# Second sequence's recurrence, projection and h2 in front of the routing list's lanes, slots and expert table

## The chip, the cores and the metric

The kernel runs on one core of a Trainium2 chip. A core has TensorE (PE, matmuls), VectorE (DVE), ScalarE (ACT), GpSimd (POOL) and SyncE (SP, here only a queue that issues DMAs). Each engine works through its own instructions in order and waits on semaphores for the others; all data that they share lies in one on-chip memory, and matmul results in eight banks of PSUM. The metric is the device time of one execution in microseconds, as the median of several runs.

## What is computed

One block with two branches over the same normalised input. Cut to what matters (x is 4 x 512 x 256; 8 experts; 2 picked for each token):

```python
xn = layernorm(x)
# branch 1: gated recurrence, then a feed-forward net
h = rmsnorm(xn); a = sigmoid(h @ w_a + bias); i = sigmoid(h @ w_i); v = h @ w_v
signal = sqrt(1 - a*a) * (i * v)
state[t] = a[t] * state[t-1] + signal[t]          # chunked scan along the sequence
x1 = xn + state @ out_proj_w
h2 = rmsnorm(x1); gate, up = split(h2 @ w_gate_up)
branch1 = x1 + (silu(gate) * up) @ w_down
# branch 2: top-2 of 8 experts for each of the 2048 tokens
logits = xn @ w_router; top-2 and their softmax
branch2 = sum over the picked e of  p_e * (square(relu(xn @ w_fc[e])) @ w_proj[e])
out = x + branch1 + branch2
```

## The kernel before

**Precision.** Nearly every matmul is made of three: each fp32 matrix is split into a rounded "hi" and a remainder "lo", and hi*hi, lo*hi and hi*lo are added in PSUM. Where a weight is split, ACT writes hi (`weights_hi`, L729) and DVE writes lo (`weights_lo`, L1184). For pieces 6 to 10 of the weights the lo half is made without DVE: ACT writes -hi into lo (L731), and a DMA issued on POOL adds the raw weight from DRAM on top (`weights_whole(n)`, L1449). Pieces 6 to 8 are the second halves of w_gate_up and w_down, 9 and 10 the first half of w_fc (Wfc).

**Stages.** The four sequences (b = 0 to 3) first pass through the recurrence's gates (`aiv`), routing logits and statistics. Then come 32 FFN tiles d = 0 to 31, eight for each sequence. A tile is `gate_up(d, 0)` and `gate_up(d, 1)` on PE (12 matmuls of 128x512), Silu on ACT (`gate`, L817), a product on DVE (`up`, L1189, signals `gu_ready`), a split into hi on ACT (`split_gu`, L837) and lo on DVE (L1194), and `down(d)` on PE (12 matmuls of 128x256), one tile later. With tile 8 (`FIRST`) the 39 expert blocks begin to be interleaved; each gathers 128 token rows by an indirect DMA on POOL (`gather`, L1455), transposes them (L615), and multiplies with Wfc and Wpj of its expert. FC, the first product of a block, is called `layer(FC, ...)` in `expert_out(i)`.

**Routing list.** DVE makes it: `blocks(k)` (L1149, L1151), `lanes(0..3)` (L1160), and `experts()` (L1165 to L1170) build comparison matrices; PE multiplies them in `slots()` (L472, 32 small matmuls into bank 6); `block_list()` (L1176, L1178) turns the result into `gather_u` and signals `routed`. POOL waits for `routed` and then issues, in this order, the gathers of blocks 0 to 3 and `weights_whole(10)`. SP waits for it to load the last piece of w_proj, which ACT and DVE split ahead of their part of block 0. PE's first FC, that of block 0, waits for `routed`, for the lo half of the row block (`xg_split`) and for both `w_whole[9]` and `w_whole[10]`.

**Second sequence.** Before tile 8 the second sequence needs `cumulate` and `recur` on DVE (L1056 to L1062), `output_projection(1, ..)` on PE (L444), `add_residual` on DVE (L1070), `squares` on ACT, `root_h2(1)` on POOL (L1423, L1424), `normalise` on ACT (L797), `transpose_h2(1, ..)` on PE (L457) and `split_h2(1)` on ACT and DVE (L1077). Sequence 1 is consumed from tile 8 on.

**What sets the order.** Every engine's program is a list written out by hand. On PE three constants place the extra work of tiles 0 to 7: behind the `gate_up` of tile `SLOTS` stands `slots()`, behind the `down` that follows tile `PROJECT_1` the second sequence's projection, behind that of `TURN_1` its transposes. Two of them share PSUM bank 6 with `slots()`, so a wait keeps them apart: before, the projection waits for `routed`.

Of the kernel before, what the change touches and what calls it, by code (L numbers as in the profile page):

```python
# [14 lines left out]
P = 128  # L15
# [21 lines left out]
def recurrent_moe_block(nc, x, pre_norm_w, w_a, w_i, w_v, out_proj_w, decay_bias, ffn_norm_w,  # L37
                        w_gate_up, w_down, w_router, w_fc, w_proj, out):
    B, S, D = x.shape
    E = w_router.shape[1]  # L40
    FF = w_down.shape[0]
    K = D // P
# [6 lines left out]
    N = T * P  # L49
    ROW = D + E  # L50
# [6 lines left out]
    xh_dram = nc.dram_tensor("xh_dram", [N + P, ROW], F32, kind="Internal").ap()  # L57
# [6 lines left out]
    with ExitStack() as ctx:  # L64
# [215 lines left out]
        PROJECT = {11: 2, 17: 3}  # L280
        TURN = {13: 2, 20: 3}

        SLOTS, PROJECT_1, TURN_1 = 3, 4, 6

        def aside(b):

# [42 lines left out]
        def _(sp):  # L329
# [3 lines left out]
            def load_piece(n):  # L333
                sp.dma_start(pieces[n][1][2], pieces[n][0]).then_inc(w_loaded[n], 16)
# [17 lines left out]
            sp.dma_start(acc_dram[1].rearrange("(n p) d -> p n d", p=P),  # L352
                         zero[:, None, 0:D].to_broadcast([P, T + 1, D])).then_inc(zero_stored, 16)
            sp.dma_start(acc_dram[0][0:N], x.rearrange("b s d -> (b s) d")).then_inc(x_copied, 16)
            sp.wait_ge(w_tok_ready, 1)
            sp.dma_start(xh_dram[0:N, D:ROW].rearrange("(t p) e -> p t e", p=P), w_tok[:, :, :]).then_inc(w_tok_stored, 16)
            sp.wait_ge(aiv_done, 6 * B)
            for n in range(UNDER_SCAN, UNDER_ROUTING):
                load_piece(n)
            sp.wait_ge(routed, 1)  # L360
            sp.wait_ge(experts_ready, 1)
            for n in range(UNDER_ROUTING, ALL):
# [11 lines left out]
        def _(pe):  # L374
# [55 lines left out]
            def output_projection(b, side):  # L430

                if side == 0:
                    pe.wait_ge(rec_ready, K * (b + 1))
                    if b == 0:
                        pe.wait_ge(wo_loaded, 16)
                        pe.wait_ge(hT_split, K * B)
                    elif b == 1:
                        pe.wait_ge(routed, 1)
                        pe.wait_ge(count_taken, 1)
                    else:  # L440
                        pe.wait_ge(*[(gu_ready, d + 1) for d in PROJECT if PROJECT[d] == b][0])
# [22 lines left out]
                nc.tensor.matmul(ps[:, 7, E * T:2 * E * T], ones_bf[:, :], bothv, start=True, stop=True).then_inc(count_done, 1)  # L464

            def slots():
                pe.wait_ge(gu_ready, 3)
                for k in range(TOP):
                    pe.wait_ge(block_ready, k + 1)
                    pe.wait_ge(lane_ready, 2 * k + 2)  # L470
                    for n in range(k * T, (k + 1) * T):
                        last = nc.tensor.matmul(ps[:, 6, 0:NB + 1], at_lane[:, n, :], id_block[:, n, :],  # L472
                                                start=n == 0, stop=n == TOP * T - 1)
                last.then_inc(slots_done, 1)
# [239 lines left out]
        def _(act):  # L714
# [217 lines left out]
            gate(3)  # L932
            weights_hi(9)
            split_gu(3)
            weights_hi(10)
            gate(4)
            weights_hi(11)
            split_gu(4)
            squares(1)
            gate(5)  # L940
            split_gu(5)
            normalise(1)
            weights_hi(12)
            gate(6)
            weights_hi(13)
            split_gu(6)
            split_h2(1)
            weights_hi(14)
            gate(7)
            weights_hi(15)  # L950
# [43 lines left out]
        def _(dve):  # L994
# [294 lines left out]
            split_h2(0)  # L1289
            gated_value(2, 0)  # L1290
            gated_value(2, 1)
            blocks(0)
            blocks(1)
            weights_lo(5)
            gated_value(3, 0)
            lanes(0)
            lanes(1)
            up(0)
            gated_value(3, 1)
            lanes(2)  # L1300
            split_gu(0)
            up(1)
            lanes(3)
            split_gu(1)
            cumulate(1, 0)
            recur(1, 0)
            up(2)
            experts()
            split_gu(2)
            cumulate(1, 1)  # L1310
            up(3)
            block_list()
            recur(1, 1)
            split_gu(3)
            up(4)
            signal(2, 0)
            split_gu(4)
            add_residual(1, 0)
            add_residual(1, 1)
            signal(2, 1)  # L1320
            signal(3, 0)
            up(5)
            signal(3, 1)
            split_gu(5)
            weights_lo(11)
            up(6)
            weights_lo(12)
            split_gu(6)
            weights_lo(13)
            split_h2(1)  # L1330
            weights_lo(14)
            up(7)
            weights_lo(15)
# [52 lines left out]
        def _(pool):  # L1386
# [101 lines left out]
            root_q()  # L1488
            tables()
            root_h2(0)  # L1490
            token_weights()
            for n in range(6, 10):
                weights_whole(n)
            pool.wait_ge(routed, 1)
            for c in range(B):
                pool.wait_ge(xh_stored[c], 16)
# [2 lines left out]
            for i in range(XG):  # L1499
                gather(i)  # L1500
            weights_whole(10)
            root_h2(1)
            pool.wait_ge(x_copied, 16)
            for d in range(FIRST, LAST + 1):
                for v, i in enumerate(blocks_of(d)):
# [52 lines left out]
```

## Time and profile before

| | us |
|---|---|
| median of 3 runs (302.01 to 303.77) | 302.41 |
| the profiled execution | 301.88 |
| its span, first to last instruction | 300.1 |
| PE busy | 282.0 (94%) |
| DVE busy | 194.6 (65%) |
| ACT busy | 170.5 (57%) |
| POOL busy | 158.0 (53%) |

The profile comes from one execution, and its span lies 1.8 us below that execution's own time. The chain that ended last is given to PE for 79% of the span, to DVE for 11% and to DMA for 2%. A timeline row gives start, duration, engine, line, operation and shapes, and in brackets the idle time before it with what ended it. A row may cover several like instructions (x2, x16); matmuls overlap, so what one costs PE is the distance between starts, not its duration. DVE's and ACT's instructions overlap by about 0.1 us in the same way.

### The profile page before, as it was taken

The page shows a single profiled execution, that of the slowest core. Times are in us where ns is not written, and L with a number is a line of the kernel's source. Part 1 is how long each engine was busy: PE and PEld are TensorE (multiplying, and loading weights), DVE is VectorE, ACT ScalarE, POOL GpSimd, SP SyncE. Part 2 cuts the span into 40 slices and gives each one's busy share as a digit, 9 for nine tenths or more (in the row PEclk, how much of TensorE's full clock was granted, in tenths as well). Part 3 has the DMA queues.
Part 4 walks back from the last instruction along what each step waited for, and adds up shares of the span by engine and source line. Part 5 has one row for each costly group of instructions (what it writes and reads, how often), then busy time and mean ns, then how long its engine had stood idle before and what let it go on. Part 6 is the DMA issues. An engine that isn't in the chain of part 4 may idle for free.

```text
span 300.1 us, 5629 instructions
## 1 busy us (share of the span) xinstructions
PE 282.0 (94%) x1826; PEld 249.5 (83%) x1826; DVE 194.6 (65%) x456; ACT 170.5 (57%) x364; POOL 158.0 (53%) x148
## 2 busy tenths in 40 slices
PE   6798999999799899999999999899998999999993
PEld 5587988887689698998988998799988999888893
DVE  3877999979967968865546578645544545443242
ACT  2677868996757744544666454436466555533330
POOL 4797002243561024776676778656876666646500
PEclk9999999999999999999999999999999999999998
DMA  6999990019982010344344353443345344529998
GB/s 174 356 374 382 383 349 0 0 13 261 189 212 41 0 30 28 63 67 70 53 74 69 60 81 62 60 66 56 70 75 76 69 73 54 56 32 161 192 197 292
DMA packets 33371, 36.91 MB, mean 123 GB/s; under 512 B 5184, under 2 KB 30528, under 8 KB 33312
## 3 DMA queue, kind: packets, MB, share of 16 engines
q0 software_dynamic: 13840, 17.20, 35.6%
q1 hardware_dynamic: 16576, 17.25, 17.1%
q10 hardware_dynamic: 2928, 2.10, 2.1%
q8 instruction: 16, 0.26, 0.3%
q14 instruction: 11, 0.09, 0.1%
HBM read 24.68 MB, written 13.96 MB: 129 GB/s over the span
## 4 chain that ended last, share of the span: by engine, by line
PE 79%; DVE 11%; issue 3%; ACT 2%; DMA 2%; SPq 1%; DVEq 0%
PE ps L376 67%; PE ps L615 5%; PE ps L444 5%; DMA X<-in_L_attn_x_dram 2%; ACT h L797 2%; DVE Wpj_lo L1184 2%; DVE gu L1189 1%; DVE guT_lo L1194 1%; PE ps L390 1%; DVE h2T_lo L1077 1%; DVE cum L1057 1%; DVE hT_lo L1031 1%; PE ps L457 1%; DVE gi L1060 1%; DVE stats L1003 0%
## 5 line engine op out<-in xcount | busy, mean ns | idle before, releaser
L1455 POOL DMA_INDIRECT xg<-xh_dram,gather_u x39 | 46.5, 1191 | 52.5 <-DVE picks L1234 40.8
L1464 POOL DMA_INDIRECT acc_dram<-yb,gather_u x39 | 62.2, 1595 | 16.3 <-issue 8.5
L376 PE MATMUL ps<-h2T_lo,Wgu_hi 128*128 128x512 f32 (+1 forms) x132 | 42.9, 386 | 0.0
L376 PE MATMUL ps<-h2T_hi,Wgu_hi 128*128 128x512 f32 (+1 forms) x132 | 41.1, 392 | 1.3 <-DVE h2T_lo L1077 0.9
L376 PE MATMUL ps<-h2T_hi,Wgu_lo 128*128 128x512 f32 (+1 forms) x132 | 40.1, 385 | 0.0
L376 PE MATMUL ps<-Wd_hi,guT_hi 128*128 128x256 f32 x128 | 36.4, 284 | 2.5 <-DVE guT_lo L1194 2.5
L376 PE MATMUL ps<-Wd_hi,guT_lo 128*128 128x256 f32 x128 | 36.2, 283 | 0.0
L376 PE MATMUL ps<-Wd_lo,guT_hi 128*128 128x256 f32 x128 | 36.1, 282 | 0.0
L1251 DVE TENSOR_TENSOR aT_lo<-ps,aT_hi 128x256 fp32r<-128x256 f32 x39 | 16.5, 424 | 29.9 <-ACT aT_hi L859 29.5
L1189 DVE TENSOR_TENSOR gu<-gu,ps 128x512 f32<-128x512 f32 x31 | 21.2, 685 | 21.1 <-PE ps L376 19.0
L817 ACT ACTIVATE gu<-ps 128x512 f32<-128x512 f32 x31 | 18.4, 594 | 22.5 <-PE ps L376 22.4
L376 PEld LDWEIGHTS ps<-h2T_lo,Wgu_hi 128*128 128x128 f32 x132 | 24.5, 188 | 4.7
L376 PEld LDWEIGHTS ps<-h2T_hi,Wgu_lo 128*128 128x128 f32 x132 | 24.5, 188 | 4.5
L837 ACT ACTIVATE guT_hi<-gu 128x512 fp32r<-128x512 f32 x31 | 19.5, 628 | 15.3 <-DVE gu L1189 15.3
L376 PEld LDWEIGHTS ps<-Wd_hi,guT_hi 128*128 128x128 f32 x128 | 24.3, 190 | 4.6 <-DVE guT_lo L1194 3.5
L859 ACT ACTIVATE aT_hi<-ps 128x256 fp32r<-128x256 f32 x39 | 14.9, 382 | 21.8 <-PE ps L615 21.8
L1242 DVE TENSOR_TENSOR xgT_lo<-ps,xgT_hi 128x256 fp32r<-128x256 f32 x39 | 16.4, 421 | 15.6 <-ACT xgT_hi L845 15.5
L845 ACT ACTIVATE xgT_hi<-ps 128x256 fp32r<-128x256 f32 x39 | 14.9, 383 | 18.5 <-PE ps L615 18.5
L376 PEld LDWEIGHTS ps<-Wd_lo,guT_hi 128*128 128x128 f32 x128 | 24.3, 190 | 1.0
L1194 DVE TENSOR_TENSOR guT_lo<-gu,guT_hi 128x512 fp32r<-128x512 f32 x31 | 21.3, 687 | 5.8 <-ACT guT_hi L837 5.4
L376 PEld LDWEIGHTS ps<-h2T_hi,Wgu_hi 128*128 128x128 f32 x132 | 21.6, 189 | 3.4 <-DVE h2T_lo L1077 1.4
L376 PEld LDWEIGHTS ps<-Wd_hi,guT_lo 128*128 128x128 f32 x128 | 24.3, 190 | 0.0
(184 smaller groups left out, 679.3 us busy)
## 6 DMA issues: line engine op xcount, KB each, us to landing
X<-acc_dram POOLq DMA_DIRECT2D x8, 512.0 KB, 10.8
acc_dram<-zero SPq DMA_DIRECT2D x1, 2176.0 KB, 16.3
Wgu_raw<-in_L_attn_w_gate_up_dram SPq DMA_DIRECT2D x4, 512.0 KB, 9.4
Wfc_raw<-in_L_ffn_w_fc_dram SPq DMA_DIRECT2D x4, 512.0 KB, 13.6
xh_dram<-X ACTq DMA_DIRECT2D x4, 512.0 KB, 7.8
Wpj_raw<-in_L_ffn_w_proj_dram SPq DMA_DIRECT2D x4, 512.0 KB, 5.5
X<-in_L_attn_x_dram SPq DMA_DIRECT2D x3, 512.0 KB, 7.2
out_dram<-X SPq DMA_DIRECT2D x3, 512.0 KB, 5.4
```

Of the source, the lines that this page charges most:

```text
L376: return nc.tensor.matmul(dst, lhs, rhs, start=start, stop=stop, skip_group_check=group)
L444: last = nc.tensor.matmul(ps[:, aside(b) + side, (j % 2) * D:(j % 2 + 1) * D], dec[b][:, k, j * P:(j + 1) * P], Wo[:, k, :], start=k == 0, ...
L615: last = nc.tensor.transpose(ps[:, bank, k * P:(k + 1) * P], src[:, k * P:(k + 1) * P], ident[:, :])
L817: A.activation(gu[d % 2][:, :], ps[:, gu_bank(d), :], ACT.Silu).then_inc(sg_ready, 1)
L837: A.activation(guT[d % 2][0][:, :], gu[d % 2][:, :], ACT.Copy).then_inc(gu_hi, 1)
L845: A.activation(xgT[i % 2][0][:, :, :].rearrange(flat), ps[:, T1, 0:D], ACT.Copy).then_inc(xg_hi, 1)
L1189: V.tensor_tensor(gu[d % 2][:, :], gu[d % 2][:, :], ps[:, gu_bank(d) + 1, :], ALU.mult).then_inc(gu_ready, 1)
L1194: V.tensor_tensor(guT[d % 2][1][:, :], gu[d % 2][:, :], guT[d % 2][0][:, :].bitcast(F32), ALU.subtract).then_inc(gu_split, 1)
L1242: V.tensor_tensor(xgT[i % 2][1][:, :, :].rearrange(flat), ps[:, T1, 0:D], xgT[i % 2][0][:, :, :].rearrange(flat).bitcast(F32), ALU.subtrac ...
L1251: V.tensor_tensor(aT[i % 2][1][:, :, :].rearrange(flat), ps[:, T2, 0:D], aT[i % 2][0][:, :, :].rearrange(flat).bitcast(F32), ALU.subtract) ...
L1455: pool.indirect_dma_start(out=xg[i % XG][:, :], out_offset=None, in_=xh_dram, in_offset=bass.IndirectOffsetOnAxis(ap=gather_u[:, i:i + 1], ...
L1464: pool.indirect_dma_start(out=acc_dram[i % 2], in_=yb[i % YB][:, :], in_offset=None, compute_op=ALU.add, out_offset=bass.IndirectOffsetOnA ...
```

## The change

The routing list moves back and the second sequence forward. On PE the projection of sequence 1 goes behind tile 3 (from 4), its transposes behind tile 5 (from 6), and `slots()` behind tile 6 (from 3). Bank 6 is now first the projection's: it waits for `gu_ready` 3 in place of `routed`, and `slots()` waits for the four halves of h2T. DVE's, ACT's and POOL's lists follow; SP stores the token weights behind three of the four w_proj loads. No arithmetic is added or taken away. The diff, with its repeated lines cut:

```diff
-        SLOTS, PROJECT_1, TURN_1 = 3, 4, 6
+        SLOTS, PROJECT_1, TURN_1 = 6, 3, 5
...
                     elif b == 1:
-                        pe.wait_ge(routed, 1)
+                        pe.wait_ge(gu_ready, 3)
...
             def slots():
-                pe.wait_ge(gu_ready, 3)
+                pe.wait_ge(h2T_split, 2 * K)
...
-            blocks(0)
-            blocks(1)
             weights_lo(5)
             gated_value(3, 0)
-            lanes(0)
-            lanes(1)
+            cumulate(1, 0)
+            recur(1, 0)
             up(0)
...
             token_weights()
-            for n in range(6, 10):
-                weights_whole(n)
+            root_h2(1)
+            weights_whole(9)
             pool.wait_ge(routed, 1)
...
             weights_whole(10)
-            root_h2(1)
             pool.wait_ge(x_copied, 16)
```

On DVE, what stands from the third FFN product on to the list. In these rows gu, guT are tiles of the FFN, L1056 to L1062 the recurrence, L1165 to L1170 `experts()`, L1176 and L1178 `block_list()`. Before:

```order
L1189 TENSOR_TENSOR gu_130<-gu_130,ps 128x512
L1165 TENSOR_TENSOR past<-blk_end,lane 128x320
L1167 TENSOR_REDUCE expert_f<-past 128x40
L1168 TENSOR_SCALAR expert_u<-expert_f 128x40
L1169 TENSOR_SCALAR one_of<-past 128x40
L1170 TENSOR_TENSOR one_of<-past 128x40x7
L1194 TENSOR_TENSOR guT_lo<-gu_130,guT_hi 128x512
L1056 TENSOR_SCALAR dec_106<-dec_106 128x512
L1057 SCALAR_TENSOR_TENSOR cum<-restart,dec_106 128x512
L1189 TENSOR_TENSOR gu_131<-gu_131,ps 128x512
L1176 TENSOR_SCALAR row_of<-ps,lane_p 128x40
L1178 SCALAR_TENSOR_TENSOR gather_u<-ps,row_of 128x40
```

The same engine in the changed kernel, from the third product to the split of that tile:

```order
L1189 TENSOR_TENSOR gu_130<-gu_130,ps 128x512
L1060 SCALAR_TENSOR_TENSOR gi_110<-cum,gi_110 128x512
L1062 SCALAR_TENSOR_TENSOR dec_106<-dec_106,gi_110 128x512
L1149 TENSOR_TENSOR at_block<-step_64,hi_f 128x640
L1151 TENSOR_TENSOR id_block<-at_block,token 128x640
L1194 TENSOR_TENSOR guT_lo<-gu_130,guT_hi 128x512
```

And, three tiles later, from the product of tile 5 to the list and what follows it:

```order
L1189 TENSOR_TENSOR gu_131<-gu_131,ps 128x512
L1077 SCALAR_TENSOR_TENSOR h2T_lo<-ps,ffn_w,h2T_hi 128x512 x2
L1194 TENSOR_TENSOR guT_lo<-gu_131,guT_hi 128x512
L1047 SCALAR_TENSOR_TENSOR gi_111<-gain_134,gi_111 128x512 x2
L1176 TENSOR_SCALAR row_of<-ps,lane_p 128x40
L1178 SCALAR_TENSOR_TENSOR gather_u<-ps,row_of 128x40
L1047 SCALAR_TENSOR_TENSOR gi_112<-gain_135,gi_112 128x512 x2
L1189 TENSOR_TENSOR gu_130<-gu_130,ps 128x512
L1184 TENSOR_TENSOR Wfc_lo<-Wfc_raw,Wfc_hi 128x1024
L1194 TENSOR_TENSOR guT_lo<-gu_130,guT_hi 128x512
L1184 TENSOR_TENSOR Wfc_lo<-Wfc_raw,Wfc_hi 128x1024
L1184 TENSOR_TENSOR Wpj_lo<-Wpj_raw,Wpj_hi 128x1024 x2
```

The recurrence now stands ahead of all the list's work, and the list (L1176, L1178) has gone from between the products of tiles 3 and 4 to just ahead of the product of tile 6.

On PE, around `slots()` in the changed kernel (L457 are the transposes of sequence 1, the rows behind it one side of tile 6 and the next, L472 `slots()`):

```order
L457 MATMUL ps<-ident_52,h2_187 128x128 x8
L376 MATMUL ps<-h2T0_hi_126,Wgu_hi_89 128x512 x2
L376 MATMUL ps<-h2T0_lo_127,Wgu_hi_89 128x512 x2
L376 MATMUL ps<-h2T0_hi_126,Wgu_lo_90 128x512 x2
L376 MATMUL ps<-h2T0_hi_126,Wgu_hi_89 128x512 x2
L376 MATMUL ps<-h2T0_lo_127,Wgu_hi_89 128x512 x2
L376 MATMUL ps<-h2T0_hi_126,Wgu_lo_90 128x512 x2
L472 MATMUL ps<-id_block_142,at_lane_140 128x40 x32
L376 MATMUL ps<-Wd_hi_92,guT1_hi_138 128x256
```

Before, `slots()` stood three tiles earlier, with neither projection nor transposes ahead of it.

On POOL, the difference between the two lists ahead of the gathers (L1432 to L1438 are `token_weights()`, L1423 and L1424 `root_h2(1)`, L1449 the adding DMAs):

```order
+L1449 DMA Wgu_lo<-in_L_attn_w_gate_up_dram 128x2x512 x2
+L1449 DMA Wd_lo<-in_L_attn_w_down_dram 128x4x256
 L1432 TENSOR_TENSOR prob<-prob,q_77 128x16 x2
 L1435 TENSOR_TENSOR tmp<-mask,prob 128x128
 L1436 TENSOR_TENSOR lg_146<-mask,prob 128x128
 L1438 TENSOR_TENSOR w_tok<-tmp,lg_146 128x128
-L1449 DMA Wgu_lo<-in_L_attn_w_gate_up_dram 128x2x512 x2
-L1449 DMA Wd_lo<-in_L_attn_w_down_dram 128x4x256
+L1423 TENSOR_SCALAR sn<-ssq 128x4
+L1424 TENSOR_TENSOR rn_88<-sn,minus_half 128x4
 L1449 DMA Wfc_lo<-in_L_ffn_w_fc_dram 128x4x256
 L1455 DMA xg_169<-xh_dram,gather_u 128x264
```

The token weights and the root now stand between the adding DMAs. Behind these rows nothing moved: the gathers of blocks 0 to 3 and then the second Wfc_lo DMA, `weights_whole(10)`, all behind `routed`.

## Rows read from the trace of the kernel before

**Rows 1.** Busy time by stretch: PE, PEld, DVE, ACT, POOL, clock, DMA share, GB/s

```profile
66.00:105.00 39.00, 35.17 (x226) 29.90 (x225) 33.84 (x50) 27.46 (x46) 13.19 (x11) 1.00 0.63 136
...
105.00:110.00 5.00, 5.00 (x39) 4.69 (x38) 2.74 (x10) 1.80 (x5) 1.09 (x1) 1.00 0.10 29
```

**Rows 2.** Chain of waits, 66 to 106 us: start, us, what

```profile
101.18 0.60 DVE gu L1189
101.77 2.27 DVE Wpj_lo L1184 x2
104.05 0.34 DVE xgT_lo L1242
```

**Rows 3.** ScalarE's timeline, 66 to 74 us: start, us, operation, idle before

```profile
69.43 0.63 ACT L837 ACTIVATE guT_hi<-gu 128x512 fp32r<-128x512 f32 x1 [1.89 <-DVE gu L1189]
...
71.87 0.57 ACT L817 ACTIVATE gu<-ps 128x512 f32<-128x512 f32 x1
```

**Rows 4.** VectorE's timeline, 56 to 81 us

```profile
56.45 0.82 DVE L1149 TENSOR_TENSOR at_block<-step,hi_f 128x640 f16<-128x640 f16 x1
...
58.05 0.82 DVE L1149 TENSOR_TENSOR at_block<-step,hi_f 128x640 f16<-128x640 f16 x1
...
66.38 0.69 DVE L1042 TENSOR_TENSOR gi<-gi,ps 128x512 f32<-128x512 f32 x1 [1.01 <-PE ps L376]
...
72.77 0.69 DVE L1060 SCALAR_TENSOR_TENSOR gi<-cum,gi 128x512 f32<-128x512 f32 x1
...
74.63 0.66 DVE L1189 TENSOR_TENSOR gu<-gu,ps 128x512 f32<-128x512 f32 x1
...
79.74 0.25 DVE L1176 TENSOR_SCALAR row_of<-ps,lane_p 128x40 f32<-128x40 f32 x1
80.03 0.20 DVE L1178 SCALAR_TENSOR_TENSOR gather_u<-ps,row_of 128x40 uint32<-128x40 f32 x1
```

**Rows 5.** TensorE's timeline, 75 to 105 us

```profile
75.47 0.98 PE L472 MATMUL ps<-id_block,at_lane 128*128 128x40 f16 x32
77.56 0.39 PE L376 MATMUL ps<-Wd_hi,guT_hi 128*128 128x256 f32 x1 [1.11 <-DVE guT_lo L1194]
...
84.26 3.62 PE L444 MATMUL ps<-Wo,dec 128*128 128x256 f32 x16
...
90.48 0.28 PE L376 MATMUL ps<-Wd_hi,guT_hi 128*128 128x256 f32 x1
...
94.66 0.28 PE L376 MATMUL ps<-Wd_hi,guT_hi 128*128 128x256 f32 x1
...
99.71 0.28 PE L376 MATMUL ps<-Wd_hi,guT_hi 128*128 128x256 f32 x1
...
104.52 0.51 PE L376 MATMUL ps<-Wfc_hi,xgT_hi 128*128 x2 [0.97 <-DVE xgT_lo L1242]
```

**Rows 6.** GpSimd's timeline, 80 to 88 us

```profile
80.51 1.30 POOL L1455 DMA_INDIRECT xg<-xh_dram,gather_u  x1 [0.60 <-DVE gather_u L1178]
...
86.26 1.47 POOL L1449 DMA_DIRECT2D Wfc_lo<-in_L_ffn_w_fc_dram  x1
```

**Rows 7.** DMA issues from 86.2 to 87 us: KB each, us to landing

```profile
Wfc_lo<-in_L_ffn_w_fc_dram POOLq DMA_DIRECT2D x1, 512.0 KB, 6.1
```

**Rows 8.** GpSimd's timeline later, shortest and longest gather

```profile
140.00 0.98 POOL L1455 DMA_INDIRECT xg<-xh_dram,gather_u  x1 [1.83 <-PE ps L615]
...
187.59 1.91 POOL L1455 DMA_INDIRECT xg<-xh_dram,gather_u  x1 [0.58 <-issue]
```

**Rows 9.** TensorE's timeline, 2 to 11 us

```profile
2.82 4.45 PE L380 MATMUL ps<-before,ones_bf 128*128 128x128 bf16 x40 [2.82 <-POOLq L1403]
...
9.89 0.83 PE L380 MATMUL ps<-before,ones_bf 128*128 128x128 bf16 x12
```

**Rows 10.** Busy time by stretch at the end, columns as in rows 1

```profile
295.00:295.50 0.50, 0.12 (x2) 0.00 (x0) 0.50 (x2) 0.00 (x0) 0.00 (x0) 1.00 1.03 363
...
298.50:299.00 0.50, 0.00 (x0) 0.00 (x0) 0.00 (x0) 0.00 (x0) 0.00 (x0) 0.50 0.68 236
```

More of the change, by code:

```diff
@@ L354, in _ @@
             sp.dma_start(acc_dram[0][0:N], x.rearrange("b s d -> (b s) d")).then_inc(x_copied, 16)
-            sp.wait_ge(w_tok_ready, 1)
-            sp.dma_start(xh_dram[0:N, D:ROW].rearrange("(t p) e -> p t e", p=P), w_tok[:, :, :]).then_inc(w_tok_stored, 16)
             sp.wait_ge(aiv_done, 6 * B)
@@ L359, in _ @@
                 load_piece(n)
+            sp.wait_ge(w_tok_ready, 1)
+            sp.dma_start(xh_dram[0:N, D:ROW].rearrange("(t p) e -> p t e", p=P), w_tok[:, :, :]).then_inc(w_tok_stored, 16)
             sp.wait_ge(routed, 1)
@@ L934, in _ @@
             split_gu(3)
+            squares(1)
+            gate(4)
             weights_hi(10)
-            gate(4)
+            split_gu(4)
+            normalise(1)
+            gate(5)
             weights_hi(11)
-            split_gu(4)
-            squares(1)
-            gate(5)
+            split_h2(1)
             split_gu(5)
-            normalise(1)
             weights_hi(12)
@@ L946, in _ @@
             split_gu(6)
-            split_h2(1)
             weights_hi(14)
@@ L1291, in _ @@
             gated_value(2, 1)
-            blocks(0)
-            blocks(1)
             weights_lo(5)
             gated_value(3, 0)
-            lanes(0)
-            lanes(1)
+            cumulate(1, 0)
+            recur(1, 0)
             up(0)
             gated_value(3, 1)
-            lanes(2)
             split_gu(0)
             up(1)
-            lanes(3)
+            cumulate(1, 1)
             split_gu(1)
-            cumulate(1, 0)
-            recur(1, 0)
             up(2)
-            experts()
+            recur(1, 1)
+            blocks(0)
             split_gu(2)
-            cumulate(1, 1)
+            blocks(1)
+            lanes(0)
             up(3)
[L1312 to L1317, printed above, removed]
             add_residual(1, 0)
             add_residual(1, 1)
+            split_gu(3)
+            lanes(1)
+            up(4)
+            lanes(2)
+            split_gu(4)
+            lanes(3)
+            experts()
+            up(5)
+            split_h2(1)
+            split_gu(5)
+            signal(2, 0)
             signal(2, 1)
+            block_list()
             signal(3, 0)
-            up(5)
             signal(3, 1)
-            split_gu(5)
+            up(6)
             weights_lo(11)
-            up(6)
+            split_gu(6)
             weights_lo(12)
-            split_gu(6)
             weights_lo(13)
-            split_h2(1)
             weights_lo(14)
@@ L1490, in _ @@
             root_h2(0)
+            for n in range(6, 9):
+                weights_whole(n)
             token_weights()
-            for n in range(6, 10):
-                weights_whole(n)
+            root_h2(1)
+            weights_whole(9)
             pool.wait_ge(routed, 1)
```

## The prediction, made before the changed kernel was run

> **What bounds the kernel now.** I read the busy times by stretch first. From 66 to 105 us, where tiles 0 to 7 run, PE is busy 35.17 of 39.00 us, so 3.8 us of PE idle time lie there; DVE is busy 33.84 us [rows 1]. In the next stretch PE is busy 5.00 of 5 us and DVE 2.74 [rows 1]: from the first expert block on PE alone sets the time. So the question is only when PE gets out of tiles 0 to 7, and the marker is its first FC, which starts at 104.52 us [rows 5]. Every microsecond that this start moves should move the end, since behind it there is no PE idle time that could absorb it.
>
> The chain of waits says what held that start: not a DMA and not the list, but DVE's queue, 0.60 us for a product, 2.27 us for two Wpj_lo, 0.34 us for xgT_lo [rows 2]. The list itself was early: `gather_u` ended at 80.03 + 0.20 = 80.23 us [rows 4], and the DMA issued behind the four gathers, `weights_whole(10)`, started at 86.26 us [rows 6] and landed 6.1 us later [rows 7], at 92.4 us. That left 12.1 us of slack to FC. The change spends this slack.
>
> **Part 1: the recurrence in front of the list, what it gives.** In the trace `down(2)` on PE starts at 77.56 us behind 1.11 us of waiting for guT_lo [rows 5]. In the changed order DVE takes at 66.38 us [rows 4] the same gated value, then without a lane in between guT_lo(0) and the product of tile 1, at 0.60 us each [rows 2]; the product ends at about 68.3. ACT then goes through the same pieces as before, from guT_hi(1) to the end of the third Silu, 69.43 to 71.87 + 0.57, 3.0 us [rows 3]: 71.4. So the third product starts at 71.5 in place of 74.63 [rows 4]. Behind it stand, ahead of guT_lo(2), the product itself 0.60, half a recurrence 74.63 - 72.77 = 1.86, and `blocks(0)` 58.05 - 56.45 = 1.60 [rows 4]: 75.6, guT_lo(2) ends at 76.2 and `down(2)` starts at 76.3. That is 1.3 us earlier than before. I find no wait behind it in tiles 3 to 5: the projection needs `recur(1, 1)`, over by 74, and each later guT_lo has about 1 us or more in hand.
>
> **Part 2: when the list is ready.** From `down(2)` on PE now runs, ahead of `slots()`: `down(2)`, 1.4; projection and one tile's gate_up, 90.48 - 84.26 = 6.22; a down and a gate_up, 94.66 - 90.48 = 4.18; a down, the transposes and a gate_up, 99.71 - 94.66 = 5.05 [rows 5]. Sum 16.9, so `slots()` starts at 93.2 in place of 75.47 [rows 5]. It takes 0.98 us [rows 5], some 0.1 us to DVE, and the two list instructions take 80.23 - 79.74 = 0.49 us [rows 4]. `routed` comes at 94.8, against 80.23: 14.6 us later. The new wait of `slots()` for h2T costs nothing, since a tile's gate_up, over 2.7 us, lies between the transposes and it, and DVE has both lo halves by about 92. What is queued behind the waiting `block_list()` on DVE are two signals and all the weight splits; DVE waits some 0.4 us there.
>
> **Part 3: what hangs on the list.** POOL waits for `routed`, then issues four gathers and the adding DMA. From `gather_u` to the start of that DMA the trace shows 86.26 - 80.23 = 6.03 us [rows 4, 6], then 6.1 us to landing [rows 7]. `w_whole[10]` thus comes at 94.8 + 6.0 + 6.1 = 106.9, and FC, which waits for it, starts at about 107.1. Before: 104.52. **Loss: 2.6 us.** The two bounds of the POOL term: a gather takes between 0.98 and 1.91 us in this trace [rows 8], and 0.3 us lie between two; four then take 5.1 to 8.8 us, and the DMA would be issued 5.4 to 9.1 us after `routed`. I keep 6.03, since it is these same four gathers under the same busy DVE and beside the same load of the last w_proj piece. This gives FC +2.0 to +5.7 us.
>
> On the price of that DMA the Trainium skill speaks against me. For 512 KB the row shows 6.1 us [rows 7]. "DMA: Bandwidth & Descriptors", section "Anatomy of one DMA", gives about 2.0 us fixed plus the bytes over 436 GB/s, an estimate of 3.2 us; by it the DMA would land at 104.0 and FC be held by something else, the first rival below. The trace's value decides here.
>
> **Part 4: the rest.** The token weights (POOL) now stand between adding DMAs and need `blocks(0)`, and the root of h2 stands behind them; by the count of part 1 both end near 85, about a microsecond before ACT uses the root. The store of the token weights is issued by SP behind three loads that wait only for the gates' last matmul, near 66, and is long over by 94.8. The last w_proj piece lands some 6 us after `routed`, at 101, and ACT splits it by 102, so that ACT's and DVE's part of block 0 is behind it but ahead of 105. These edits cost nothing as long as `w_whole[10]` is later; without that cover they are the first rival. PE's time saved in part 1 is given back in the wait before FC and is in the sum already. PE's work is unchanged.
>
> **Sum.** Profiled execution 301.88 us, span 300.1, plus 2.6: 304.5. The median of the runs shown is 302.41, 0.53 us above that execution: 305.0 us.
>
> **Rivals.**
>
> *A. The adding DMA is hidden, and DVE's queue decides as before.* Behind `gather_u` DVE still has five instructions of 0.60 us and six weight splits of 2.27 / 2 = 1.14 us, then xgT_lo 0.34 us [rows 2]: 94.8 + 3.0 + 6.8 + 0.3 = 104.9, and FC 0.13 us later, at 105.1, or 0.6 us later than before. Time 303.0. For it: DVE is busy for 87% of this stretch already, and its work is only reordered. Against it: POOL's path would have to be 2 us shorter than the same instructions took in the trace.
>
> *B. PE's clock falls in the new wait.* By DVE's queue the last gate_up ahead of FC ends at about 103.9, so PE stands still for some 3.2 us before 107.1. At the end of the trace PE's last matmul ends at 295.1 with the granted clock at 1.00, and from 298.5 on the granted clock is 0.50, 1.2 of 2.4 GHz [rows 10]. What a low level costs: 40 small matmuls at the start take 4.45 us, 12 of the same later 0.83 us [rows 9], 111 ns against 69 ns each, so 1.7 us over a ramp of that length. Time 305.0 + 1.7 = 306.7. The Trainium skill's "TensorE: Matmul & The Clock Gate", section "Why this matters for your kernels", asks for no longer idle gaps between bursts of matmuls, since the clock then goes back to half; the rows at the end of the trace agree.
>
> *C. Faster.* If neither POOL nor DVE holds FC, PE comes to it by its own work: `slots()` ends at 94.2, a down and a gate_up 4.18, then what lay between 99.71 and 104.52 without the last wait of 0.97 us [rows 5], 3.84 us: 102.2, which is 2.3 us earlier. Time 300.1. It decides only if `w_whole[10]` has landed by 102.2, within 7.4 us of `routed`, where the trace shows 12.1, and if DVE has also caught up 3 us.
>
> **How the numbers follow.** Forecast 0.68, A 0.15, B 0.12, C 0.05. A measurement of this kernel can tell about 0.5%, 1.5 us, from no change: 300.9 to 303.9. The forecast and B are slower by more, A is within it, C is faster; I move 0.02 from slower to the middle for a `routed` that comes a microsecond earlier than my count. Faster 0.05, same 0.17, slower 0.78. The range starts a little under A, 302.8, and goes to 307.9, which holds B and nearly the upper bound of the gathers (305.0 + 3.1); C and rows beyond that are left out.
>
> **What would show it.** In the changed profile: `down(2)` near 76.3; L472 near 93.2; `gather_u` near 94.8; the L1449 DMA behind the fourth gather near 100.8; FC near 107, its idle time put down to that DMA or, since a wait is named by what came last, to an engine long done; the stretch from FC on busy on PE as before, and a span near 302.7. If PE's idle time ahead of FC is under 1.5 us and xgT_lo ends right before it, A was right. If small matmul spacings behind FC are doubled, B. If `routed` comes before 90, part 2 is wrong, and with it all else.

## The result: 310.5 us, 2.3% slower, beyond the range

The changed kernel takes 310.51 us in the median of 4 runs (308.77 to 311.19), beside 302.37 us (302.01 to 303.77) for the kernel before. The ratio is 1.0227, with a 95% interval of 1.0176 to 1.0278. It is slower, as forecast, but by 8.1 us where 2.6 were forecast, and the time lies above the range.

The profiled execution took 310.57 us, its span is 308.5 us, 8.4 us over the span before. Two of the changed kernel's waits of TensorE between 60 and 125 us (what waited and for whom: us in total, times, longest):

```profile
PE ps L376 <- DMA Wfc_lo<-in_L_ffn_w_fc_dram: 4.4, 1, 4.4
...
PE ps L376 <- DVE gu L1189: 2.2, 1, 2.2
```

The first is new, for the adding DMA, ahead of FC. The second stands ahead of the last gate_up before FC; the kernel before waited 0.39 us for the same product at this place. The chain of waits between 90 and 116 us shows what the first is made of:

```profile
96.03 0.84 PE ps L472 x32
...
97.19 0.21 DVE gather_u L1178
...
97.69 1.29 POOL xg L1455
...
99.28 1.92 POOL xg L1455
...
101.50 1.44 POOL xg L1455
...
103.24 1.96 POOL xg L1455
105.20 5.66 DMA Wfc_lo<-in_L_ffn_w_fc_dram
110.86 0.34 issue
111.20 2.90 PE ps L376 x9
```

`slots()` (L472), the list (L1178), four gathers (L1455), the DMA of 5.66 us, and then TensorE. In the kernel before, the same stretch of the chain was VectorE's queue [rows 2]. TensorE's own timeline of the changed kernel, against [rows 5] of before:

```profile
61.93 0.62 PE L376 MATMUL ps<-h2T_hi,Wgu_hi 128*128 128x512 f32 x2
```

```profile
78.89 0.39 PE L376 MATMUL ps<-Wd_hi,guT_hi 128*128 128x256 f32 x1 [1.05 <-DVE guT_lo L1194]
...
95.87 0.98 PE L472 MATMUL ps<-id_block,at_lane 128*128 128x40 f16 x32
...
105.13 0.70 PE L376 MATMUL ps<-h2T_hi,Wgu_hi 128*128 128x512 f32 x2 [2.18 <-DVE gu L1189]
...
111.20 0.76 PE L376 MATMUL ps<-Wfc_hi,xgT_hi 128*128 x2 [4.45 <-DMA Wfc_lo<-in_L_ffn_w_fc_dram]
```

The first row is the surprise. Tile 0 starts at 61.93 us, where it started at 59.31 us in the kernel before, and nothing that the change touches runs that early. So there are three losses, and each can be read off by taking the stretches apart. The first is the start: tile 0 comes 2.6 us late. The second is the stretch from tile 0 to the first FC: 111.20 - 61.93 = 49.3 us, where it was 104.52 - 59.31 = 45.2, so 4.1 us more. The third is from FC to the end of the span: 308.5 - 111.2 = 197.3, where it was 195.6, so 1.7 us more. For the first, the chain of waits of the changed kernel between 8 and 17 us begins with the load of the second sequence's input:

```profile
3.31 7.65 DMA X<-in_L_attn_x_dram
...
13.13 1.20 DVE hT_lo L1031 x2
```

In the profile of before the same piece of the chain is 6.64 us long, 1.0 us less. For the third, these are busy times by stretch, columns as in [rows 1], the granted clock the last but two:

```profile
16.00:18.00 2.00, 2.00 (x6) 1.61 (x5) 1.93 (x13) 0.90 (x2) 1.42 (x3) 0.50 1.09 359
...
111.00:112.00 1.00, 0.80 (x4) 0.80 (x5) 0.00 (x0) 0.00 (x0) 0.00 (x0) 0.63 0.00 0
112.00:113.00 1.00, 1.00 (x5) 0.95 (x5) 0.00 (x0) 0.14 (x1) 0.00 (x0) 0.50 0.00 0
113.00:114.00 1.00, 1.00 (x4) 0.65 (x3) 0.51 (x3) 0.24 (x1) 0.00 (x0) 0.50 0.00 0
114.00:115.00 1.00, 1.00 (x6) 0.88 (x5) 0.02 (x1) 0.39 (x1) 0.44 (x1) 0.66 0.00 0
115.00:116.00 1.00, 1.00 (x9) 0.95 (x8) 0.94 (x2) 0.00 (x0) 0.61 (x1) 1.00 0.00 0
```

At 16 and at 112 us the granted clock stands at 0.50, 1.2 of 2.4 GHz; the first time behind a wait of 2.00 us of TensorE for hT_lo, the second behind the waits ahead of FC. So a clock fall belongs to the start too. An estimate from the four rows of 111 to 115 us: what they lack of full speed adds up to 0.37 + 0.50 + 0.50 + 0.34 = 1.7 us, which is the third loss. The runs below take these three losses apart.

### The profile page after: what moved, and what is told of

The parts are those of the page before. It is cut to its first block, busy times and chain, and to the rows that moved or that the text cites. A ratio compares the mean times of both kernels' runs of the same rounds, so it can differ in the third digit from the quotient of the medians.

```text
span 308.5 us, 5630 instructions
## 1 busy us (share of the span) xinstructions
PE 284.9 (92%) x1826; PEld 251.9 (82%) x1826; DVE 194.0 (63%) x456; ACT 170.7 (55%) x364; POOL 160.0 (52%) x148
## 4 chain that ended last, share of the span: by engine, by line
PE 76%; ACT 7%; DVE 5%; DMA 4%; issue 3%; POOL 2%; SPq 1%; DVEq 0%; ACTq 0%
PE ps L376 65%; PE ps L615 5%; PE ps L444 4%; DMA X<-in_L_attn_x_dram 2%; POOL xg L1455 2%; DMA Wfc_lo<-in_L_ffn_w_fc_dram 2%; ACT h L797 1%; PE ps L390 1%; PE ps L457 1%; ACT gain L785 1%; DVE hT_lo L1031 1%; ACT gain L780 1%; ACT Wgu_hi L729 1%; ACT h2T_hi L805 1%; DVE h2T_lo L1077 0%
## 5 line engine op out<-in xcount | busy, mean ns | idle before, releaser
L1455 POOL DMA_INDIRECT xg<-xh_dram,gather_u x39 | 48.2, 1237 | 53.3 <-DVE picks L1234 25.8
L1247 DVE TENSOR_TENSOR act_e<-ps,act_e 128x256 f32<-128x256 f32 x39 | 16.6, 425 | 14.9 <-ACT act_e L865 11.2
L865 ACT ACTIVATE act_e<-ps 128x256 f32<-128x256 f32 x39 | 15.0, 386 | 18.2 <-PE ps L376 15.8
```

Of the source, the lines that this page charges most:

```text
L865: A.activation(act_e[i % 2][:, :], ps[:, FC, 0:D], ACT.Relu).then_inc(relu_done, 1)
L1247: V.tensor_tensor(act_e[i % 2][:, :], ps[:, FC, 0:D], act_e[i % 2][:, :], ALU.mult).then_inc(act_ready, 1)
L1455: pool.indirect_dma_start(out=xg[i % XG][:, :], out_offset=None, in_=xh_dram, in_offset=bass.IndirectOffsetOnAxis(ap=gather_u[:, i:i + 1], ...
```

## The experiments

Since executions differ by up to 3 us at the start, traces are compared by three marks: the start of tile 0 on TensorE, the start of the first FC (Wfc_hi, xgT_hi), and the end of the span. The kernel before has 45.2 us between the first two and 195.6 us between the last two in its first trace; in a second one, below, they are 45.2 and 196.0, so a difference of 0.4 us behind FC says nothing.

### The kernel before once more

> The kernel before, unchanged, for a second trace beside the others of this call. In the first trace of the changed kernel everything up to tile 0 already ran 2.66 us late: the load of X of the second sequence landed 1.0 us later, TensorE stood still 2.00 us ahead of hT_lo in place of 0.90, and its clock was 0.50 from 16 to 18 us. Theory S (start-up varies from run to run): in this trace too the second product of lo weights may start anywhere from 13.3 to 14.4 us, and the clock of 16 to 18 us may be 1.00 or 0.50. Theory C (the changed program causes it): this trace repeats 13.3 us and a clock of 1.00.

305.32 us and a span of 303.5. The input load of its chain took 7.42 us, 0.8 us more than in the first trace; one short VectorE instruction behind it (L1008) took 0.77 us in place of 0.17. And TensorE's timeline at the start reads:

```profile
12.07 0.63 PE L376 MATMUL ps<-hT_hi,Waiv_lo 128*128 128x512 f32 x2
14.69 0.73 PE L376 MATMUL ps<-hT_lo,Waiv_hi 128*128 128x512 f32 x2 [1.98 <-DVE hT_lo L1031]
...
16.63 1.06 PE L376 MATMUL ps<-hT_lo,Waiv_hi 128*128 128x512 f32 x2
```

The wait on hT_lo is 1.98 us, as in the changed kernel, and the two matmuls at 16.63 take 1.06 us in place of 0.62: the clock. Tile 0 starts at 62.29 us and FC at 107.50, 45.2 us behind; from there to the end it takes 196.0 us. Theory S holds: the late start happens without the change too. In 13 runs of the kernel before that stood beside these it took 302.09 to 305.3 us.

### The changed kernel once more

> The changed kernel, unchanged, timed against the kernel before. Theory S: the time lies between 306 and 311 us and the start-up differs between its executions. Theory C: 310.5 us again, with hT_lo's product at 14.4 us and a clock of 0.50 from 16 to 18 us. Both expect the first FC 14 us behind gather_u (111.20 - 97.39 = 13.8 in the first trace).

310.62 us (308.99 to 311.87), ratio 1.0259 with an interval of 1.0204 to 1.0315. This time the trace has tile 0 at 59.87 us, nearly on time, FC at 109.46, 49.6 us behind it, and the end 197.4 us behind FC. The adding DMA was again issued 7.8 us behind the list, and FC came 6.3 us behind that in place of 6.0. So 4.1 to 4.4 us up to FC and 1.7 to 1.9 us behind it (1.3 to 1.5 against the second trace of before) belong to the change, and a start that is late by 0 to 3 us does not. The expectation's 13.8 us from the list to FC became 109.46 - 95.31 = 14.2.

### e1: the adding DMA ahead of the wait for the list

```diff
             weights_whole(9)
+            weights_whole(10)
             pool.wait_ge(routed, 1)
...
                 gather(i)
-            weights_whole(10)
```

> The changed kernel with one step moved: weights_whole(10), the adding DMA on Wfc's second piece, is issued on GpSimd ahead of the wait for routed, right behind weights_whole(9), in place of behind the four gathers. Main theory (FC waits for that DMA, and the wait costs 4.4 us and lets the clock fall once): FC starts right behind xgT_lo, at the place DVE's queue sets, some 3.6 us earlier relative to gather_u than in the changed kernel (10.2 us behind it), and the clock stays at 1.00 there, worth another 1.5 us. Time 5 us below the changed kernel, some 305.5. Rival (FC is held by the gathers or by the last w_proj piece as well): under 2 us gained.

304.95 us (302.67 to 307.17), ratio 1.006 with an interval of 1.0021 to 1.0098; 5.7 us under the changed kernel in the medians. In the traces, from tile 0 to the end, it is 244.0 against 246.6 and 247.0 us, 2.5 to 3.0 us less; the rest of the 5.7 is not taken apart here, and the start varies in both. FC in this trace:

```profile
102.36 0.70 PE L376 MATMUL ps<-h2T_hi,Wgu_hi 128*128 128x512 f32 x2 [2.17 <-DVE gu L1189]
...
104.96 0.79 PE L376 MATMUL ps<-Wfc_hi,xgT_hi 128*128 x2 [0.75 <-DVE xgT_lo L1242]
```

It starts at 104.96 us, 45.8 us behind tile 0 (59.16), right behind xgT_lo, and the DMA is gone from its wait. This is rival A of the prediction, to the tenth: VectorE's queue then sets FC, 0.6 us later than in the kernel before. The second half of the expectation failed. The clock fell all the same:

```profile
102.00:103.00 1.00, 0.64 (x3) 0.58 (x4) 1.00 (x2) 0.63 (x1) 0.44 (x1) 1.00 0.00 0
103.00:104.00 1.00, 1.00 (x5) 0.47 (x3) 1.00 (x2) 0.00 (x0) 0.00 (x0) 0.80 0.49 135
...
105.00:106.00 1.00, 1.00 (x5) 1.00 (x6) 0.42 (x1) 0.00 (x0) 0.00 (x0) 0.50 0.00 0
...
109.00:110.00 1.00, 1.00 (x5) 0.90 (x4) 0.49 (x2) 0.00 (x0) 0.29 (x1) 0.50 0.12 25
110.00:111.00 1.00, 1.00 (x9) 1.00 (x8) 0.39 (x1) 0.01 (x1) 0.00 (x0) 0.79 0.42 126
```

It is at 1.00 until 103, falls there and stays at 0.50 until 110, and from FC to the end it takes 198.2 us, 2.6 more than before. The only idle time of TensorE of more than 0.1 us between 92 us and the fall is the 2.17 us ahead of the last gate_up before FC; the 0.75 us for xgT_lo come behind the fall. So the wait for the DMA is not needed for the clock to fall: it can fall right behind the gap of 2.2 us in front of it, which the changed kernel has too. In the seven traces with neither this gap nor a wait for the DMA (before twice, e3, e4, e6, e7, e8) the clock did not fall there. Of the six traces with this gap of 2.2 us the clock fell before FC in three (here, and below in e9 and e10), behind the DMA's wait in two (the changed kernel's), and not at all in e2.

### e2: unused matmuls in the wait

`keep_clock(56, 7)` puts 56 matmuls of 128 columns, whose result nobody reads, into PSUM bank 7 ahead of the waits of FC.

```diff
                     else:
+                        keep_clock(56, 7)
                         pe.wait_ge(routed, 1)
```

> The changed kernel with 56 small matmuls of 128 columns, whose result is not used, on TensorE ahead of the first FC's wait for the adding DMA. They take about 3.1 us at full clock and fit in the wait. Main theory: FC starts when it did (13.8 us behind gather_u), but the stretch behind it runs at 1.00 in place of 0.66, and the time falls by 1.5 to 1.7 us. Rival (the clock in that stretch is not what costs): no change within 0.5 us.

309.38 us (307.21 to 310.21). In the trace FC comes 109.18 - 59.23 = 49.95 us behind tile 0, a little later than without them (49.3 to 49.6), and the end only 195.9 us behind FC, where the changed kernel took 197.3 and 197.4. The clock is at 1.00 through 105 to 115 us. The medians differ by 1.2 us, but the times of the two kernels overlap (4 runs each), and the start may be a part of it; the traces give 1.4 to 1.5 us for the clock behind FC, less the 0.4 to 0.7 by which FC came later. The matmuls do not show as the cause of that delay: behind them TensorE still waited 0.94 us for the DMA, which landed 6.3 us after its issue, where the changed kernel had 5.7 and 6.0. Why it took longer is open.

### e3: the DMA early and VectorE's splits later

On VectorE the product of tile 7 and xgT_lo of block 0 move ahead of the four Wpj splits; with e1's edit:

```diff
             weights_lo(12)
-            weights_lo(13)
-            weights_lo(14)
             up(7)
-            weights_lo(15)
-            weights_lo(16)
...
+                        if i == 0:
+                            weights_lo(13)
+                            weights_lo(14)
                         if v == 1:
                             up(d)
+                        if i == 1:
+                            weights_lo(15)
...
                         block_weight(i)
+                        if i == 1:
+                            weights_lo(16)
```

> The changed kernel with two edits: weights_whole(10) ahead of the wait for routed, as in the run before, and on VectorE the product of tile 7 and xgT_lo of block 0 ahead of the four Wpj splits, which follow inside blocks 0 and 1. Main theory (with the DMA out of the way FC is set by VectorE's queue): FC starts at TensorE's own arrival, 42 to 43 us behind tile 0 (changed kernel 49.3 to 49.6, kernel before 45.2), the 2.2 us of idle time ahead of gate_up(8) go, the clock stays at 1.00, and the time is 299 to 300.5 us, under the kernel before. Rival (ScalarE's w_proj pieces or the gathers come next): FC at 44 to 46 us behind tile 0 and 302 us or more.

302.72 us (302.34 to 306.7), ratio 1.001 with an interval of 0.9961 to 1.0058. FC starts at 102.58 us, 42.5 us behind tile 0 (60.06), 2.7 us sooner than in the kernel before: TensorE's own arrival, which the prediction's rival C had put at 102.2 - 59.3 = 42.9. The idle time ahead of gate_up(8), the last before FC, is gone and the clock stays at 1.00 there. But the end comes 198.3 us behind FC, 2.7 more than before, so the whole gain is given back:

```profile
109.98 0.47 PE L376 MATMUL ps<-Wpj_hi,aT_hi 128*128 x2 [1.70 <-DVE Wpj_lo L1184]
```

The first PJ now waits 1.70 us for the last Wpj split, and the rest of what was given back lies in the gaps just ahead of it, where VectorE is busy without a pause. Only part of the main theory held.

### e4: VectorE's edit on the kernel before

> The kernel before with the VectorE edit alone: product of tile 7 and xgT_lo of block 0 ahead of the four Wpj splits. If VectorE's queue alone set the first FC there, as its chain of waits says, FC comes at most 2.3 us earlier (42.9 us behind tile 0) and the time falls to 300.5 to 301.5. If the splits are then late for the first PJ, the gain is given back there and the time stays at 302.5 to 303.

304.27 us (302.83 to 307.01), ratio 1.0035 with an interval of 0.9997 to 1.0072: no gain. FC 43.5 us behind tile 0 and the end 198.1 us behind FC: 1.7 us gained, 2.5 given back, with a wait of 1.69 us of the first PJ for Wpj_lo. Both expectations were too kind; the chain of waits named VectorE, and relieving its queue at one place loaded it at the next.

### e5: VectorE's edit on the changed kernel, the DMA left where it is

> The changed kernel with the VectorE edit alone; the adding DMA stays behind the four gathers. FC has to wait for that DMA as before. Theory P (VectorE's two-input splits slow the issue of the gathers on GpSimd, 1.92 and 1.96 us in the changed kernel against 0.95 to 1.43 before): with four splits of 1.2 us gone from that stretch the later gathers take 0.95 to 1.3 us, the adding DMA is issued 6.0 us behind gather_u in place of 7.8 to 8.0, and FC comes 12.2 us behind it in place of 13.8 to 14.1. Rival (the gathers' price has another cause): 7.8 to 8.0 us and 13.8 us again.

310.02 us in two runs. What it is for are the gathers, and this is GpSimd's timeline:

```profile
95.07 1.29 POOL L1458 DMA_INDIRECT xg<-xh_dram,gather_u  x1 [8.46 <-DVE gather_u L1178]
96.66 1.92 POOL L1458 DMA_INDIRECT xg<-xh_dram,gather_u  x1 [0.30 <-issue]
98.88 1.44 POOL L1458 DMA_INDIRECT xg<-xh_dram,gather_u  x1 [0.30 <-issue]
100.62 0.95 POOL L1458 DMA_INDIRECT xg<-xh_dram,gather_u  x1 [0.30 <-issue]
101.57 1.47 POOL L1452 DMA_DIRECT2D Wfc_lo<-in_L_ffn_w_fc_dram  x1
```

The first three gathers are the same as in the changed kernel's chain above, 1.29, 1.92 and 1.44 us; the fourth takes 0.95 us in place of 1.96. What VectorE did beside the gathers, first in the changed kernel (from the second gather on) and then here (beside the fourth):

```profile
99.11 1.22 DVE L1184 TENSOR_TENSOR Wfc_lo<-Wfc_raw,Wfc_hi 128x1024 fp32r<-128x1024 f32 x1
...
100.89 1.22 DVE L1184 TENSOR_TENSOR Wfc_lo<-Wfc_raw,Wfc_hi 128x1024 fp32r<-128x1024 f32 x1
102.03 2.35 DVE L1184 TENSOR_TENSOR Wpj_lo<-Wpj_raw,Wpj_hi 128x1024 fp32r<-128x1024 f32 x2
104.30 0.68 DVE L1189 TENSOR_TENSOR gu<-gu,ps 128x512 f32<-128x512 f32 x1
104.90 2.35 DVE L1184 TENSOR_TENSOR Wpj_lo<-Wpj_raw,Wpj_hi 128x1024 fp32r<-128x1024 f32 x2
```

```profile
99.41 0.68 DVE L1189 TENSOR_TENSOR gu<-gu,ps 128x512 f32<-128x512 f32 x1
101.26 0.42 DVE L1242 TENSOR_TENSOR xgT_lo<-ps,xgT_hi 128x256 fp32r<-128x256 f32 x1 [1.17 <-ACT xgT_hi L845]
```

In the changed kernel a pair of 1024-wide splits, with two inputs in on-chip memory, ends inside the fourth gather (103.24 to 105.20), and the next pair begins inside it; here VectorE stands idle for 1.17 us ahead of xgT_lo, which covers the fourth gather (100.62 to 101.57) but for its last 0.3 us. The adding DMA is issued 101.57 - 94.77 = 6.8 us behind the list in place of 105.20 - 97.39 = 7.8. Theory P expected 6.0; the fourth gather fell as it said, and the second stayed at 1.92 us, because a split still runs at its start. FC comes 13.2 us behind the list in place of 13.8. But with VectorE's work out of the way TensorE is sooner at its wait and stands in it for 6.15 us, the clock is at 0.50 until past FC by 4 us, and the first PJ waits 1.36 us for its weights, much as in e3: the end comes 199.8 us behind FC, 4.2 more than before, so that the time is no lower.

The rows allow more than "VectorE is busy". The second gather starts at 99.28, inside a split that ends at 99.11 + 1.22 = 100.33, 1.05 us later, and takes 1.92; the third starts at 101.50 with 0.61 us of a split left and takes 1.44, though splits run beside all of it; the fourth has 1.14 us left of one and takes 1.96. So what counts is how much is left of the instruction that VectorE is in when the gather starts. All 546 gathers of the 14 traces fit this. Where VectorE was idle at their start, or in an instruction with an input in PSUM, they took 0.94 to 1.09 us (354). Where it was in one with two inputs that both lie in the on-chip memory (192), they took 0.95 us and what was left of it less 0.1 us, each within 0.14 us. By it the changed kernel's four gathers had 0.30, 1.05, 0.61 and 1.14 us left at their starts, those of the kernel before 0.31, 0.55, 0.33 and nothing:

```profile
82.11 1.43 POOL L1455 DMA_INDIRECT xg<-xh_dram,gather_u  x1 [0.30 <-issue]
...
85.31 0.95 POOL L1455 DMA_INDIRECT xg<-xh_dram,gather_u  x1 [0.30 <-issue]
```

Less 0.1 us each, these add 0.89 us to four times 0.95 us before and 2.70 us in the changed kernel. The difference, 1.8 us as an estimate, is the 1.8 us by which the DMA was issued later.

### e6: the start

On the kernel before, the split of the first hT goes ahead of the second sequence's statistics, which wait for a load:

```diff
             normalise_first(1)
-            statistics(1)
             split_h(0)
+            statistics(1)
             split_router()
```

> The kernel before with hT_lo's split of the first sequence ahead of the second sequence's statistics on VectorE. Theory (start-up spread: the statistics wait for a load that lands 1 us earlier or later, TensorE waits behind them, and its clock falls in some executions): hT_lo's product starts at 12.5 us, its wait is under 0.5 us, and the spread of the times shrinks from 302.0 to 305.3 to under 1.5 us, median about 301.5 to 302.5. Rival (the spread comes from elsewhere): the spread stays at 3 us.

301.56 us (301.18 to 302.92), ratio 0.9934 with an interval of 0.9899 to 0.9969. The same place in the trace:

```profile
11.85 0.63 PE L376 MATMUL ps<-hT_hi,Waiv_lo 128*128 128x512 f32 x2
12.31 0.63 PE L376 MATMUL ps<-hT_lo,Waiv_hi 128*128 128x512 f32 x2
```

No wait is left ahead of the lo product, where it was 0.90 to 2.00 us, and 25 runs of the kernel before beside it spread from 302.06 to 306.0 us, this one's ten from 301.18 to 302.92. The theory holds, with a spread of 1.7 us where it expected under 1.5. The fall that goes with a late tile 0 is the late one: the granted clock stood at 0.50 somewhere between 15 and 19 us in the two traces that had tile 0 at 61.9 and 62.3 us. A fall between 9 and 14 us, in the second trace of the changed kernel, in e3, e4, e5 and, in spite of this edit, in e7, went with tile 0 at 58.8 to 60.1 us.

### e9 and e10: the change without the start's spread

> The changed kernel with the start edit alone. The kernel before with it took 301.56 us (301.18 to 302.92). Theory: what the change itself costs is 4.2 us at the first FC and 1.6 us of clock behind it, 5.8 in all, and the rest of the 8 us measured is start-up: 307.3 us, with a spread under 2 us. Rival (the change costs 8 us by itself): 309.5 us.

308.21 us (307.91 to 309.06, 4 runs), 6.65 us over e6, the kernel before with the same edit. The two were timed on different occasions; the kernel before beside them had medians of 302.84 and 303.14 us, so some 0.3 us of this is unsure. In the traces, tile 0 to FC takes 49.65 us against 45.21, 4.4 more, and FC to the end 197.7 against 195.7, 2.0 more. The clock had fallen at 102 us already, ahead of the wait for the DMA. So the change costs 6.4 to 6.7 us by itself, between the theory's 5.8 and the rival's 8.

> The changed kernel with the start edit and the 56 unused matmuls ahead of the first FC. It prices the clock without the spread of the start: 1.5 us under the run just before, 305.8 us. Rival (the clock costs nothing by itself): the same time as the run just before.

307.24 us (306.14 to 309.35), 1.0 us under e9, with overlapping times. Here the unused matmuls began at half clock already and took 4.18 us in place of the 3.1 that they were sized for:

```profile
104.61 4.18 PE L380 MATMUL ps<-before,ones_bf 128*128 128x128 bf16 x56 [0.46 <-DVE xgT_lo L1243]
108.78 0.51 PE L376 MATMUL ps<-Wfc_hi,xgT_hi 128*128 x2
```

FC came 0.2 us later for it behind tile 0 than in e9, and the end 1.3 us sooner behind FC.

### e7 and e8: a version that beats both, with either order

e7 is the changed kernel with three edits: e1's, e6's, and VectorE's splits spread so that one stands ahead of xgT_lo of block 0, two behind guT_lo(7) and one in block 1:

```diff
             weights_lo(12)
-            weights_lo(13)
-            weights_lo(14)
             up(7)
-            weights_lo(15)
-            weights_lo(16)
+            weights_lo(13)
...
+                        if i == 0:
+                            weights_lo(14)
+                            weights_lo(15)
                         if v == 1:
                             up(d)
+                        if i == 1:
+                            weights_lo(16)
```

> The changed kernel with three edits: the adding DMA ahead of the wait for routed; VectorE's Wpj splits spread, one ahead of xgT_lo of block 0 (where VectorE stood still 1.17 us), two behind guT_lo(7) and one in block 1, so that the first PJ waits less than 1.70 us; and the split of the first hT ahead of the second sequence's statistics. If these are the costs found so far, they add up: span 300.9 of the run with both queues, less 1.1 at PJ and 1.3 at the start, 298.5, time 300.3, under both kernels by 0.7% or more. If the PJ wait is refilled by another one: 301.5.

300.76 us (300.43 to 301.24), ratio 0.9905 with an interval of 0.987 to 0.994: the fastest kernel of this study. FC 42.5 us behind tile 0, the end 197.1 us behind FC, still 1.5 us more than before: the first PJ comes 5.93 us behind FC, where it was 4.94 us. Its chain between 90 and 112 us names no engine but TensorE, in 19 pieces five of which are:

```profile
92.89 0.82 PE ps L472 x32
93.71 5.87 PE ps L376 x36
...
99.79 3.18 PE ps L376 x15
...
105.11 1.71 PE ps L376 x12
...
107.23 2.48 PE ps L376 x12
```

> The kernel before with the same order of VectorE's Wpj splits and the same start, but its own order of recurrence and list. It tells whether the change is of any use once its DMA is out of the way. Theory (the recurrence in front is worth the 1.3 us at down(2) minus what the list gives back): 301 us, 0.5 to 1 us above the run just before. Rival (the order of list and recurrence makes no difference then): within 0.3 us of it.

301.26 us (300.74 to 301.9), ratio 0.9941 with an interval of 0.9912 to 0.9969. FC 43.5 us behind tile 0, the end 196.7 behind FC, a span of 299.0 against 298.4. So with the DMA out of its way the changed order is ahead of the old one by 0.5 us in the medians and 0.6 in the spans. The times of the two overlap (300.43 to 301.24 in 7 runs, 300.74 to 301.9 in 10), and so do their intervals against the common kernel before, so this last step is likely and not shown.

## Why the prediction was right in its mechanism and wrong in its size

**Right.** Relative to tile 0 the steps up to the list came out to the tenth. `down(2)`: forecast 76.3 - 59.3 = 17.0, measured 78.89 - 61.93 = 17.0. `slots()`: 33.9 and 33.9. The list: 94.8 - 59.3 = 35.5, and 97.39 - 61.93 = 35.5. FC waits for `w_whole[10]`, as said, and e1, which takes only that wait away, moves FC to the place given for rival A.

**The term that was too small** is the POOL term of part 3. From the list to the issue of the adding DMA I took 6.03 us from the kernel before, on the ground that the same four gathers run "under the same busy DVE". They took 7.8 us in both traces of the changed kernel. A gather's time depends on what VectorE is in the middle of when it starts (e5): before, the second and third gather began inside 512-wide instructions and the fourth beside an idle VectorE, 1.43, 1.16 and 0.95 us; behind the late list stand the 1024-wide weight splits, and they took 1.92, 1.44 and 1.96. That the splits are the cause is tested for the fourth alone, which is 1.0 of the 1.8 us; for the others it rests on the agreement of the 546 gathers. The upper bound that I had drawn, 9.1 us, would have covered it; the value inside the bounds was chosen by the wrong likeness. The landing was nearly right, 5.66 + 0.34 us against 6.1 and 0.2. So FC came 4.1 us later in place of 2.6: 1.5 us, made of 1.8 for the gathers less 0.3 for the landing, of the 5.8 us by which the span missed its forecast. The other parts are 1.7 us of clock and 2.6 us of start. The Trainium skill's estimate in part 3 ("DMA: Bandwidth & Descriptors", section "Anatomy of one DMA"), 3.2 us for that DMA, is not borne out: 5.7 us here, 6.1 before.

**The step that was a rival and should have been a term** is B. I gave it 0.12 and weighed it against the forecast, though it needs the forecast's own wait and adds to it. In all four traces in which FC waited for the DMA and nothing filled the wait, the clock was at 0.50 when FC had started: the two of the changed kernel, e5 and e9, though in e9 it had fallen at 102 us, ahead of that wait, behind the gap of 2.2 us. Its price was forecast at 1.7 us; measured are 1.7, 1.9 and 2.0 between FC and the end in the changed kernel's two traces and e9. That the size agrees is luck. It was taken from two batches of small matmuls at the start, of 111 and 69 ns apiece, and the granted clock of the kernel before reads 1.00 in every slice from 3 to 11 us, so no row shows the slower batch to be a low level of the clock. The prediction named one wait ahead of FC where there were two: the gap of 2.2 us ahead of the last gate_up, where before there were 0.39 us, was in no part of the sum. It cost nothing by itself as long as FC waited for the DMA, but behind it the clock fell in e1, e9 and e10.

**What the prediction did not know of** is the start. The median of the kernel before stood near the fast end of its own spread, 302.0 to 306.0 us over all runs, and I had three runs and one trace of it. Without the start's spread the change costs 6.65 us in the medians, 6.2 in the spans: 4.4 up to FC, 2.0 behind it, less 0.2 by which tile 0 happened to start sooner. The rest of the 8.1 us, some 1.5, is the difference between what the start edit is worth on the changed kernel (310.51 to 308.21, 2.3 us) and on the kernel before (302.37 to 301.56, 0.8 us; 1.6 against the median of the 25 later runs). Whether the changed program starts late more often, or eight runs of it fell that way, stays open.

**Rivals A and C** were no outcome of the change but good figures of what lay behind it: A's 45.8 us from tile 0 to FC is e1's, C's 42.9 is e3's and e7's 42.5. What C left out is what comes after: e3 reached C's place and had given it all back once the first PJ had started.

**My marks.** Of the signs named, `down(2)`, L472, `gather_u` and FC's releaser came as written, shifted by the start, and the low clock behind FC, B's mark, came as well; the DMA was issued at 105.2 in place of 100.8, which is 1.8 us later by its own doing and 2.6 by the start. The span was 308.5 and not 302.7.

## What to carry to other kernels

When a producer is moved later, list everything issued behind its signal on every queue, and price that queue by what its neighbours will be doing at the new time, not at the old one: here a DMA that never needed the list stood behind it, and moving that one line gave back 5.7 us in the medians, about 3 of them from tile 0 to the end. When a forecast contains a new wait of TensorE like the one here (4.0 to 6.2 us, and each time the clock fell at it or just ahead of it), the fall belongs into the sum and not among the rivals. And before a change of 1% is judged, look at where two traces of the same kernel differ: a swing of 1 us in one load at the start went with up to 3 us at the end, with the fall of the clock behind it, more than the change was forecast to cost.

## What the runs showed of the hardware that was not expected

- The granted clock fell in e1 at about 103.6 us, behind a single idle time of TensorE of 2.17 us that had ended at 102.36; it stayed at 0.50 from 104 to 110 us, longer than in the changed kernel (112 to 114), whose wait was longer. In e2, with the same gap, it did not fall. The Trainium skill's "TensorE: Matmul & The Clock Gate" (section "Why this matters for your kernels") warns of long idle gaps; here the clock fell within 1.3 us behind one gap of 2.2 us in three traces (e1, e9, e10) and did not in a fourth (e2).
- A gather on GpSimd takes 0.95 us with VectorE idle at its start, 1.43 us in e7 with 0.61 us of a wide two-input split left, and 1.96 us with 1.14 us left. The Trainium skill's "SBUF — State Buffer" (section "SBUF: two separate sides") says that the two engines share a port pair which one holds for a whole instruction; these rows and the 546 gathers counted under e5 agree with that. The issue of the adding DMA, also on GpSimd, does not show it: 1.47 us with VectorE idle (86.26 us, before) and 1.49 us begun inside a split (105.20 us, changed kernel). No run here separated the port from other causes.
- The same 512 KB adding DMA took 5.7, 6.0, 6.1 and 6.3 us in different traces and, issued right behind another one in e1, a median of 7.2 us for the two.
